# Finishing pieces spread over batches 1 to 8, routing pieces moved into batches 14 and 15, and products of constants on TensorE

## The reference, cut to what matters

```
x = x + 0.5 * ffn(layernorm(x))      # mixture of 8 experts, the top 2 per token
x = x + attention(layernorm(x))      # 16 heads of 8 values, softmax over 256 keys
x = x + 0.5 * ffn(layernorm(x))      # the same experts again

# ffn: scores = softmax(x @ gate.T); the 2 experts with the largest scores + bias
#      rows, each scaled by its score, sorted by expert;
#      h = silu(xe @ w1[e]) * (xe @ w3[e]); out = h @ w2[e], added back per token
# attention: q, k, v = x @ W; softmax(q k / sqrt(8)) @ v, then @ Wo
```

## Time and profile before

| | before |
|---|---|
| median of 3 runs | 765.34 us (761.83 to 770.02) |
| the profiled execution's own time | 765.52 us |
| its span | 763.7 us |
| mean granted TensorE clock | 0.929 of full |
| busy: PE / DVE / ACT / POOL | 623.9 / 445.6 / 389.8 / 303.2 us |

### The profile page before, as it was taken

How to read it: one execution, slowest core, us unless ns; L and a number is a source line. 1 busy time by engine, 2 the same in 40 slices (tenths; PEclk the granted TensorE clock), 3 DMA queues, 4 the chain that set the end, 5 groups by cost and what they waited for, 6 DMA issues and landing times.

```text
span 763.7 us, 14753 instructions
## 1 busy us (share of the span) xinstructions
PE 623.9 (82%) x4966; PEld 465.6 (61%) x4966; DVE 445.6 (58%) x1163; ACT 389.8 (51%) x910; POOL 303.2 (40%) x313
## 2 busy tenths in 40 slices
PE   5248999999988788889889998888999989999200
PEld 5237898999866334445445554344889979999200
DVE  4845753225454888898999999871567422233111
ACT  0524665444422567767777777575356544444000
POOL 6057533665433226254000010003375137777574
PEclk9999999999999779999999999776999999999655
DMA  7255888877982444535334443034478768887422
GB/s 253 69 182 147 238 245 230 227 230 211 282 245 76 140 129 121 161 112 152 114 98 130 124 135 104 2 98 155 115 197 243 238 185 231 260 243 224 112 79 62
DMA packets 116298, 126.02 MB, mean 165 GB/s; under 512 B 12480, under 2 KB 99008, under 8 KB 115968
## 3 DMA queue, kind: packets, MB, share of 16 engines
q1 hardware_dynamic: 98256, 100.15, 43.6%
q0 software_dynamic: 9088, 18.63, 9.9%
q10 hardware_dynamic: 8880, 6.30, 2.5%
HBM read 89.37 MB, written 35.39 MB: 163 GB/s over the span
## 4 chain that ended last, share of the span: by engine, by line
PE 58%; DVE 20%; DMA 6%; issue 5%; ACT 5%; POOL 5%; SPq 1%; POOLq 0%; ACTq 0%; DVEq 0%
PE banks L673 13%; PE banks L645 9%; PE banks L654 9%; PE banks L661 8%; DVE mx L805 8%; PE banks L1050 6%; POOL rows L580 4%; PE banks L467 3%; ACT PT L1064 2%; PE banks L635 2%; DMA xe<-routed_rows,idx 2%; PE banks L934 2%; PE banks L1023 2%; DMA X<-in_x 1%; DVE resid L792 1%
## 5 line engine op out<-in xcount | busy, mean ns | idle before, releaser
L560 POOL DMA_INDIRECT xe<-routed_rows,idx x156 | 151.8, 973 | 241.5 <-DVE idx L434 105.0
L805 DVE TENSOR_REDUCE mx<-banks 128x2 f32<-128x512 f32 x256 | 163.5, 684 | 9.7 <-PE banks L1025 8.6
L1064 ACT ACTIVATE PT<-banks 128x512 f32<-128x512 f32 x256 | 141.5, 604 | 48.4 <-PE banks L1036 46.2
L580 POOL DMA_INDIRECT rows<-slots_out,slot x128 | 123.3, 963 | 67.4 <-issue 27.8
L726 DVE TENSOR_TENSOR hidT<-banks,act 96x256 f32<-96x256 f32 (+1 forms) x92 | 34.9, 380 | 189.2 <-ACT act L707 188.9
L673 PE MATMUL banks<-WR,hidT 128*128 128x128 f32 x936 | 119.8, 275 | 0.6 <-ACT ye L716 0.6
L673 PEld LDWEIGHTS banks<-WR,hidT 128*128 128x128 f32 x936 | 111.9, 191 | 3.0 <-issue 1.0
L645 PE MATMUL banks<-xeT,WR 128*128 128x256 f32 (+1 forms) x368 | 87.6, 361 | 5.9 <-issue 3.0
L1023 PE MATMUL banks<-KS,QS 56*128 56x256 bf16 x256 | 70.0, 289 | 18.8 <-DVE mx L805 15.1
L654 PE MATMUL banks<-xeT,WR 128*96 128x256 f32 (+1 forms) x368 | 84.4, 352 | 0.0
L661 PE MATMUL banks<-xeT,WR 128*128 128x256 f32 (+1 forms) x368 | 83.3, 349 | 0.0
(11 more groups left out here) (156 smaller groups left out, 865.4 us busy)
## 6 DMA issues: line engine op xcount, KB each, us to landing
WR<-in_experts SPq DMA_DIRECT2D x92, 544.0 KB
stacks<-split SPq DMA_DIRECT2D x32, 384.0 KB
slots_out<-ye SPq DMA_DIRECT2D x156, 64.0 KB
QS<-stacks SPq DMA_DIRECT2D x64, 112.0 KB
KS<-stacks SPq DMA_DIRECT2D x64, 112.0 KB
routed_rows<-xn ACTq DMA_DIRECT2D x16, 256.0 KB, 5.6
routed_rows<-xn SPq DMA_DIRECT2D x12, 256.0 KB, 2.3
xe<-routed_rows,idx POOLq DMA_INDIRECT x156, 4.9
```

Of the source, the lines that this page charges most:

```text
L560: eng.indirect_dma_start(xe[:, i % XR, a, :], None, routed_rows[h], bass.IndirectOffsetOnAxis(ap=idx[h][:, tile:tile + 1], axis=0))\
L580: eng.indirect_dma_start(rows[:, k, t, :], None, slots_out[h], bass.IndirectOffsetOnAxis(ap=slot[h][:, k, t:t + 1], axis=0))\
L805: eng.tensor_reduce(mx[:, :, e, pair], maxima_bank(f)[:, :].rearrange("p (q n) -> p q n", q=2), AX.X, ALU.max).then_inc(s_max, 1)
L1064: eng.activation(PT[:, u % 4, 1 - k].rearrange("p t n -> p (t n)"), PS[f % 3], ACT.Exp, scale=scale).then_inc(s_exp2, 1)
```

## The change

Six things change, and the work for the output stays as it is.

- The finishings 5, 6 and 7 on DVE had one piece per step from steps 10, 28 and 55. Now their pieces stand in steps 8, 9, 12, 13 and 20; 16, 17, 24, 25, 32, 33 and 36; and 48, 49, 56, 57, 64, 65 and 68.
- GpSimd gathers the results of the second half for them by other counts of exponentials (`s_exp2` at least 4 instead of 24 for the first 16, 72 instead of 64 for the others), and does the power of finishing 5 inside this loop, before its eleventh gather.
- The routing of group 2 on DVE: the pieces from the reciprocal of the softmax to the choice of experts stood in steps 104 to 111 and stand in 106 to 115; the slot, one-hot and expert pieces stood in 116 to 124 and stand in 118 to 125; the last piece, `idx`, stood in step 126 and comes after the loop. `rows_vector` stood in steps 113 to 115 and stands in 124, 126, 127 and after the loop.
- ACT makes `xn` in steps 117 to 127 (twelve tiles), and the last four after `ending_scalar`'s first part; before they stood in 113 to 123. TensorE's one-hot products (line 467, 32 of them) stood in steps 122 to 124; 24 stand in steps 125 and 126, and the last 8 after `ending_tensor`'s first part.
- SP stores the rows in another order and issues the weights of loads 46 and 47 before the last four of the eight stores.
- TensorE makes a product of the identity and `WO` into the free bank 4 after each step from 118 to 127, and eight of them before the last expert block. Nobody reads them.

```diff
@@ -512,7 +512,10 @@
 
         def last_rows_sync(eng):
 
-            for k, c in ((1, 0), (1, 1), (0, 0), (1, 2), (1, 3), (0, 1), (0, 2), (0, 3)):
+            for k, c in ((0, 0), (0, 1), (1, 0), (1, 1), (1, 2), (0, 2), (1, 3), (0, 3)):
+                if (k, c) == (1, 2):
+                    weights(eng, HALVES * NL)
+                    weights(eng, HALVES * NL + 1)
                 if k == 0:
                     eng.wait_ge(s_xr, rows_made(2) + 4 * c + 4)
                     rows_store(eng, 0, 4 * c + 3, xn)
@@ -596,17 +599,18 @@
                 combine_part(eng, g, h, c)
                 yield
 
-        def expert_sync(eng, first, last, *sides):
+        def weights(eng, i):
+
+            g, l, w, row = load_of(i)
+            if l == 0:
+                eng.wait_ge(s_expert, g + 1)
+            e = eng.value_load(expert[g % HALVES][0:1, l:l + 1], min_val=0, max_val=EXPERTS - 1)
+            wait(eng, s_y, i - WRING + 1)
+            eng.dma_start(WR[:, i % WRING, :], experts[bass.ds(e, 1), :, :].squeeze(0))\
+               .then_inc(s_wl[i % WRING], 16)
+
+        def expert_sync(eng, first, last, *sides, begun=0):
             lag = 2
-
-            def weights(i):
-                g, l, w, row = load_of(i)
-                if l == 0:
-                    eng.wait_ge(s_expert, g + 1)
-                e = eng.value_load(expert[g % HALVES][0:1, l:l + 1], min_val=0, max_val=EXPERTS - 1)
-                wait(eng, s_y, i - WRING + 1)
-                eng.dma_start(WR[:, i % WRING, :], experts[bass.ds(e, 1), :, :].squeeze(0))\
-                   .then_inc(s_wl[i % WRING], 16)
 
             def rows_out(i):
                 g, l, w, row = load_of(i)
@@ -616,8 +620,8 @@
                        .then_inc(s_st[i % RING], 16)
 
             for i in range(first, last + lag + 2):
-                if i < last:
-                    weights(i)
+                if first + begun <= i < last:
+                    weights(eng, i)
                 if i - lag - 2 >= first:
                     rows_out(i - lag - 2)
                 aside(sides, i)
@@ -920,6 +924,13 @@
                     if done and u == 7:
                         project(eng, n)
                     advance(side, ticks, PAIRS * n + u)
+                    if PAIRS * n + u > PAIRS * (BATCH - 2) + 5:
+                        keep_pace(eng, 1)
+
+        def keep_pace(eng, products):
+
+            for _ in range(products):
+                eng.matmul(PS[4][:, 0:D], ident, WO[:], start=True, stop=True)
 
         def turn_values(eng, n, qt):
 
@@ -1267,10 +1278,6 @@
 
             return lambda i: sum(ticks for first, last, ticks in parts if first <= i <= last)
 
-        def from_step(first):
-
-            return lambda i: int(i >= first)
-
         @block.sync
         def _(sp):
             xv = x.rearrange("(t p) d -> p t d", p=P)
@@ -1286,7 +1293,7 @@
             expert_sync(sp, 0, HALVES * NL, (prologue_sync(sp), in_loads(NL + 14, 6), -1))
             attention_sync(sp)
             last_rows_sync(sp)
-            expert_sync(sp, HALVES * NL, 2 * HALVES * NL)
+            expert_sync(sp, HALVES * NL, 2 * HALVES * NL, begun=2)
             for h in range(HALVES):
                 for c in range(GC):
                     tiles = slice(h * TH + c * TH // GC, h * TH + (c + 1) * TH // GC)
@@ -1320,10 +1327,11 @@
                 next(outs)
                 if n == 3 * KT // 4 + 3:
                     root_gpsimd(pool, 4, 0, tiles_of_chunks(2))
-            root_gpsimd(pool, 5, 0, tiles_of_chunks(3))
             outs = gathers_out(pool, 1)
             for n in range(KT):
-                wait(pool, s_exp2, PAIRS * (3, PAIRS)[n // (KT // 2)] + 2 * (n % (KT // 2)))
+                wait(pool, s_exp2, (4, 72)[n // (KT // 2)] + 2 * (n % (KT // 2)))
+                if n == 10:
+                    root_gpsimd(pool, 5, 0, tiles_of_chunks(3))
                 next(outs)
                 if n % (KT // 2) == KT // 2 - 1:
                     c = n // (KT // 2) * 2
@@ -1357,11 +1365,11 @@
             expert_scalar(act, 0, HALVES * NL, (route_scalar(act, 1), by_load(0, SCALAR), NL - 2),
                           (ahead, by_load(1, AHEAD_SCALAR), -1), between=((ahead, by_load(1, AHEAD_SCALAR_MID), -1),))
             side = route_scalar(act, 2)
-            attention_scalar(act, side, spans((103, 103, 17), (113, 113, 23), (114, 119, 1), (120, 123, 2), (124, 124, 1)))
-            for _ in side:
-                pass
+            attention_scalar(act, side, spans((105, 105, 17), (117, 117, 23), (118, 127, 1)))
             ending = ending_scalar(act)
             next(ending)
+            for _ in side:
+                pass
             expert_scalar(act, HALVES * NL, 2 * HALVES * NL,
                           (route_scalar(act, 3), by_load(2, BESIDE * (0,) + SCALAR), 3 * NL - 2),
                           (ending, by_load(2, (0, 1, 1)), -1), between=((ending, by_load(2, (1, 0, 0, 1)), -1),))
@@ -1381,11 +1389,12 @@
                 pass
             pe.wait_ge(s_ye, HALVES * NL)
             side = route_tensor(pe, 2)
-            attention_tensor(pe, side, spans((115, 115, 39), (122, 122, 33), (123, 125, 1)))
-            for _ in side:
-                pass
+            attention_tensor(pe, side, spans((117, 117, 39), (125, 125, 33), (126, 126, 1)))
             ending = ending_tensor(pe)
             next(ending)
+            for _ in side:
+                pass
+            keep_pace(pe, 8)
             expert_tensor(pe, HALVES * NL, 2 * HALVES * NL,
                           (route_tensor(pe, 3), by_load(2, BESIDE * (0,) + TENSOR), 3 * NL - 2),
                           (ending, by_load(2, (1, 1, 1)), -1), between=((ending, by_load(2, (1, 1, 1, 1)), -1),))
@@ -1420,16 +1429,18 @@
                 pass
             for _ in done:
                 pass
-            side = chained(route_norm(dve, 8, 0, 1), route_vector(dve, 2, 0))
+            side, made = chained(route_norm(dve, 8, 0, 1), route_vector(dve, 2, 0)), rows_vector(dve)
             attention_vector(dve, (finish(dve, 4, 0, 2), lambda i: 2 * int(2 <= i <= 4), 5),
-                             (finish(dve, 5, 0, 3), from_step(PAIRS + 2), 2 * PAIRS + 5),
-                             (finish(dve, 6, 1, 0, 1), from_step(3 * PAIRS + 4), 4 * PAIRS + 5),
-                             (finish(dve, 7, 1, 2, 3), from_step(6 * PAIRS + 7), 8 * PAIRS),
-                             (side, spans((72, 73, 1), (80, 81, 1), (88, 89, 1), (96, 96, 3), (97, 97, 1), (101, 101, 12),
-                                     (104, 106, 2), (108, 111, 1), (112, 112, 14), (116, 116, 1), (117, 119, 2),
-                                     (120, 120, 3), (121, 121, 2), (122, 123, 1), (124, 124, 2), (126, 126, 18)), None),
-                             (rows_vector(dve), spans((113, 114, 1), (115, 115, 2)), None))
-            for _ in side:
+                             (finish(dve, 5, 0, 3), spans((8, 9, 1), (12, 13, 1), (20, 20, 2)), 2 * PAIRS + 5),
+                             (finish(dve, 6, 1, 0, 1), spans((16, 17, 1), (24, 25, 1), (32, 33, 1), (36, 36, 2)),
+                              4 * PAIRS + 5),
+                             (finish(dve, 7, 1, 2, 3), spans((48, 49, 1), (56, 57, 1), (64, 65, 1), (68, 68, 2)),
+                              8 * PAIRS + 5),
+                             (side, spans((72, 73, 1), (80, 81, 1), (88, 89, 1), (96, 96, 3), (97, 97, 1), (104, 104, 12),
+                                     (106, 107, 1), (109, 109, 1), (111, 113, 1), (114, 114, 2), (115, 115, 3),
+                                     (116, 116, 13), (118, 119, 2), (120, 121, 3), (122, 123, 2), (125, 125, 2)), None),
+                             (made, spans((124, 124, 1), (126, 127, 1)), None))
+            for _ in chained(made, side):
                 pass
             second = chained(route_norm(dve, 9, 1, 1), route_vector(dve, 3, 1))
             done = combine(dve, 2, 0)
```

More of the change, by code:

```diff
@@ L1359, in _ @@
             side = route_scalar(act, 2)
-            attention_scalar(act, side, spans((103, 103, 17), (113, 113, 23), (114, 119, 1), (120, 123, 2), (124, 124, 1)))
+            attention_scalar(act, side, spans((105, 105, 17), (117, 117, 23), (118, 127, 1)))
+            ending = ending_scalar(act)
+            next(ending)
             for _ in side:
                 pass
-            ending = ending_scalar(act)
-            next(ending)
             expert_scalar(act, HALVES * NL, 2 * HALVES * NL,
@@ L1383, in _ @@
             side = route_tensor(pe, 2)
-            attention_tensor(pe, side, spans((115, 115, 39), (122, 122, 33), (123, 125, 1)))
+            attention_tensor(pe, side, spans((117, 117, 39), (125, 125, 33), (126, 126, 1)))
+            ending = ending_tensor(pe)
+            next(ending)
             for _ in side:
                 pass
-            ending = ending_tensor(pe)
-            next(ending)
+            keep_pace(pe, 8)
             expert_tensor(pe, HALVES * NL, 2 * HALVES * NL,
```

## The result

The changed kernel took 757.76 us in the median of four runs (754.46 to 759.90), the kernel before 766.3 us on the same chip (four runs, 761.83 to 770.02): ratio 0.9874, 95% interval 0.9845 to 0.9903, or 1.3% faster. The two medians alone stand 8.5 us or 1.1% apart, which lies inside that interval. The forecast was 759.5 us with a range of 751 to 769. The profiled execution took 759.9 us with a span of 758.1 us, against 763.7 before.

What follows compares the result with a forecast made beforehand. The chain of waits was 58% TensorE and 20% DVE, DVE's part in attention. Gains of 6.5 (finishings), 3.0 (batch 13) and 5.4 (batches 14, 15) less 9.0 (hand-over) made 5.9 us: 765.52 to 759.5, range 751 to 769.

Steps and rivals of the forecast that it cites:

- the room at the head of a batch: In a clean attention batch DVE waits 1.53 us in steps u = 1 and 2, so work there costs nothing.
- the excess that the forecast gave to batch 6: Steps u = 0 and 1 hold 2.1 us of DVE pieces against 1.53 of room: 0.6 us too much.
- POOL's side holds: GpSimd's gathers of the second half finish near 297 us, before the combine in step 24 at 308.
- signs of being wrong: Listed signs included combines waiting for GpSimd's gathers and TensorE gaps in batches 1 to 3 bringing the clock down.
- The size of 6.5 us: Moving finishings 5 to 7 in batches 1 to 8 gains 6.5 us, bounds 5 and 7.5.
- the allowance for a fall of the clock: Batch 13 gains 3.0 us instead of 3.4, leaving one clock fall in every second case.
- A third of the half clock left: Batches 14 and 15 to `turn_raw` keep a third of their half clock, so they gain 5.4 us.
- The build-up at full clock: Batches 14 and 15 to `turn_raw`, built from ACT at 2.4 GHz: 15.3 plus 17.5, 32.8 us.
- clock held: Rival: DVE lets TensorE go on, products fill the rest, 2.4 GHz from batch 13 on: 752.8 us, chance 0.25.
- The hand-over: From `turn_raw` to load 46's first transpose, last `xn`, store and gathers now follow in line: 9.0 us lost.
- The rival in which the hand-over decides: Last store, gathers and first transpose form one uncovered chain costing 15.4 us, plus 2.6 at half clock: 771, chance 0.13.
- the order within a ring: Engines take a ring's descriptors in order, so at the last block's start stores wait behind 1.1 MB of two weights.

Runs made afterwards that it cites:

- all together: Changed kernel with finishing 5 in steps 10 to 13, rows ready before `turn_raw`, two weights before the last four stores: ratio 0.9893 to the kernel before.

## Why the prediction was right, point by point

**Direction and size**: 5.9 us forecast, 5.6 between the profiles, 8.5 by the medians and 9.7 by the ratio. The direction and the place of each effect were right. That the total between the profiles comes so near is in part luck: the finishings gave 3.3 us less than forecast, and batches 13 to 15 with the hand-over 3.8 us more; the rest lies in stretches that had no term.

**Batches 7 and 8, the room at the head of a batch**: right. 31.5 us forecast, 30.8 measured; batches 5 and 6 took 31.1, 0.6 over the 30.5 of before, which is the excess that the forecast gave to batch 6.

**Batches 1 to 4**: the step that failed is "POOL's side holds". It was worked out for the gathers of the second half, and not for the chunk that finishing 5 itself combines, which was now wanted two steps sooner. Two of the prediction's signs of being wrong came here: a combine that waits for POOL's gather (1.69 us), and half clock where it had held, in batch 3 (0.90, 17.4 us). Batches 1, 2 and 3 grew by 1.6, 0.7 and 0.9 us, and batch 4, at full clock as forecast, gave 3.9 back: 0.6 us gained, where the forecast had them within 66 us, 3.3 under the 69.3 of before. How the clock fell in batch 3, where no wait of TensorE was over 0.7 us, was not found. On the other chips the other half of the step fails too, that moving the transfers into batch 1 costs "nothing": with the finishings moved, batches 0 and 1 are longer there by 5 to 9 us (gathers and pieces together), while batch 4 is 8 to 9 us shorter. The size of 6.5 us agrees with the 6.0 that the finishings alone gave by the runs, but not by the forecast's working.

**Batch 13**: right, 14.0 us against 14.4; the allowance for a fall of the clock was not needed.

**Batches 14 and 15**: the term was mis-sized: 7.7 us against 5.4. "A third of the half clock left" was too much; none was left. (A third of the way from its 8.3 to its 1.0 is also 5.9 us, not 5.4.) The build-up at full clock was 32.8 plus 0.5 us of late division; measured 33.9, with TensorE waiting 0.99 us for that division. Of the rivals, "clock held" describes this stretch, with the first half of its reason in batches 13 and 14 (DVE lets TensorE go on) and the second in batch 15 (the products fill the rest). In batches 13 and 14 it is the routing's new place that counts: all eleven profiles with it have 14.0 and 14.8 us at 1.00, with 1.4 us of waiting for maxima and with or without products; the three with the old place, one of them with the products, have a clock of 0.81 to 0.90 and 0.74 to 0.82 and 4.7 to 4.9 us of such waits. The pieces of DVE, ACT and TensorE moved together, so that it is DVE's pieces is read from these waits; none was tested alone. The products hold the clock in batch 15 in five profiles of nine; in the two without those in the steps it is 0.76.

**The hand-over**: the chain was right link by link, and the total near because two sizes were off in opposite ways. Forecast: last `xn` 2.85 us after `turn_raw`, store 2.9, 0.1 from its landing to GpSimd's first gather, second gather 4.5, 9.0 us lost. Measured: 2.6, 3.1, 0.9, 3.2, 8.3 us lost. `idx` was not late. The eight products did hide in it. The rival in which the hand-over decides did not come: the two weights before the last store were issued 5 us ahead of it, and it landed in 3.10 us; all together, with 2.2 us between them and a store of 6.37, shows what it would have looked like. The prediction also says that the gather of 5.64 us behind weights would agree with the order within a ring. That reading is wrong: the weights go through SP's queue and the gathers through GpSimd's, so the row says nothing on the order in one queue. Only the stores share a queue with the weights.

## What to carry to other kernels

Pieces of side work cost least where their engine waits anyway: find that place in a clean period and put them there, and check each piece's own inputs at its new time, not only those of its neighbours. Where TensorE's clock falls beside short waits, remove the waits first: here products that only keep it busy helped after that in one batch, and gave nothing before it (ratio 1.002). Work moved past the end of a stage joins a serial chain there; here a move that gained 11.5 us gave 8.3 back at the next stage's first gather.

## What the runs showed of the hardware

The kernel before took 766 us on one chip and 833 to 839 on three others. The changed kernel's profiles on the first chip and on the second (spans 758.1 and 821.5 us) show where the difference lies: 18 us before attention, 19 us in attention's batches 0 to 6, 26 us in the last block, and nothing in batches 7 to 15, which agree to 0.1 us each. In the stretch where the last block goes over to its second group, four loads (from the first transpose of load 69 to that of load 73) took 15.3 us on the first chip and 39.6 on the fourth, with TensorE busy 1.46 us of ten and the DMA share at 0.27 in the second row (stretch and length, busy us by engine, clock, DMA share, GB/s, changed kernel on the fourth chip):

```profile
655.00:665.00 10.00, 6.81 (x45) 5.70 (x43) 1.11 (x2) 1.72 (x4) 7.56 (x9) 1.00 0.61 172
665.00:675.00 10.00, 1.46 (x4) 1.22 (x5) 1.11 (x2) 0.75 (x2) 7.56 (x9) 0.56 0.27 54
```

The chain of waits of that stretch runs over a queue that the profile doesn't name, so that transfers are the slow part there is likely and not shown. Batches 13 and 14 took 14.0 and 14.8 us on every chip with the routing in its new place.
